# Two gather tiles in every three turns fetched row by row by SyncE and ScalarE

## What is computed

```python
# layer 0, for every edge e with source src[e] and destination dst[e]
w   = silu(edge_attr_64 @ fc_w1 / 8) @ fc_w2 / 8      # 224 weights for one edge
es, ev = h_s[edge_src], h_v[edge_src]                 # gathered node rows (64 + 96 numbers)
m_s1 = w1 * es * e0; m_s2 = w4 * dot(ev, e1)          # products of weight, row and edge attributes
m_v1 = w2 * es * e1; m_v2 = w3 * ev * e0; m_v3 = w5 * cross(ev, e1)
agg = segment_sum(mid, edge_dst)                      # then lin2, gates, silu
# layer 1: gather x[edge_src], products with edge_attr_4, segment_sum, linear maps W1..W5, Ws, Wv
```

## Time and profile before

| | us |
|---|---|
| median of three runs | 2017.59 |
| the profiled execution | 2016.04 |
| its span | 2014.2 |
| POOL busy in the span | 1459.9 (72%) |
| PE busy | 1695.3 (84%) |
| DVE busy | 1277.7 (63%) |
| ACT busy | 174.8 (9%) |

### The profile page before, as it was taken

The page is one execution under the profiler, slowest core; times in us unless marked ns, Lnnn a source line. Parts: engine busy times, 40 slices in busy tenths (PEclk is TensorE's granted clock), DMA queues, the critical chain, the costliest instruction groups (busy, mean ns, idle before and its releaser), DMA issues.

```text
span 2014.2 us, 41903 instructions
## 1 busy us (share of the span) xinstructions
PE 1695.3 (84%) x15596; PEld 1443.5 (72%) x15596; DVE 1277.7 (63%) x2725; ACT 174.8 (9%) x392; POOL 1459.9 (72%) x1558
## 2 busy tenths in 40 slices
PE   6989898989898989898958877878787878778786
PEld 4767676767676767676737877878787878778786
DVE  6787878787878877878875545444444545454443
ACT  5100000000000000000050000000000000000000
POOL 2777777777777777777737777777777777777774
PEclk9999999989999989989968989899998989899998
DMA  6333333333333333333322222222222223222223
GB/s 234 104 104 89 100 98 100 98 100 97 99 99 99 98 99 99 98 99 99 100 60 70 72 68 70 69 71 68 71 68 70 69 70 71 68 71 69 70 68 83
DMA packets 106120, 176.80 MB, mean 88 GB/s; under 512 B 27328, under 2 KB 73104, under 8 KB 105952
## 3 DMA queue, kind: packets, MB, share of 16 engines
q0 software_dynamic: 73200, 125.03, 25.5%
q1 hardware_dynamic: 30560, 49.88, 7.6%
q10 hardware_dynamic: 2320, 1.44, 0.2%
HBM read 170.10 MB, written 6.14 MB: 87 GB/s over the span
## 4 chain that ended last, share of the span: by engine, by line
POOL 69%; issue 22%; PE 4%; DVE 2%; DMA 1%; ACT 1%; POOLq 1%; DVEq 0%; ACTq 0%
POOL g L594 69%; PE sums L847 1%; PE w_ps L858 1%; DMA g<-node_table,src 1%; PE sums L868 1%; PE w_ps L457 1%; ACT H L268 0%; POOLq L589 0%; PE sums L858 0%; PE w_ps L812 0%; DMA node_table<-H 0%; PE w_ps L1020 0%; DVE work L721 0%; DMA ident_sb<-ident_dram 0%; PE sums L843 0%
## 5 line engine op out<-in xcount | busy, mean ns | idle before, releaser
L594 POOL DMA_INDIRECT g<-node_table,src x1525 | 1445.2, 948 | 494.8 <-issue 462.4
L847 PE MATMUL sums<-g,sel 128*128 128x160 f32 x1612 | 294.7, 344 | 178.7 <-DMA g<-node_table,src 177.4
L847 PEld LDWEIGHTS sums<-g,sel 128*128 128x128 f32 x1612 | 270.1, 223 | 195.9 <-DMA g<-node_table,src 139.9
L858 PE MATMUL w_ps<-H,work 128*128 128x160 f32 x2900 | 405.2, 300 | 2.5 <-DVE work L688 2.5
L858 PEld LDWEIGHTS w_ps<-H,work 128*128 128x128 f32 x2900 | 398.0, 191 | 2.7 <-DVE work L688 2.7
L721 DVE TENSOR_TENSOR work<-w_ps,g 128x384 f32<-128x384 f32 (+3 forms) x693 | 299.0, 459 | 114.5 <-DMA g<-node_table,src 67.7
L740 DVE STREAM_TRANSPOSE turned<-sums 128x160 f32<-128x160 f32 x232 | 80.1, 345 | 440.3 <-PE sums L868 303.5
L812 PE MATMUL w_ps<-fc_sb,work 64*128 64x224 f32 x1612 | 241.8, 398 | 89.2 <-DVE work L715 87.0
L843 PEld LDWEIGHTS sums<-work,sel 128*32 128x32 f32 x6448 | 202.6, 114 | 115.1 <-issue 78.0
L812 PEld LDWEIGHTS w_ps<-fc_sb,work 64*128 64x128 f32 x1612 | 173.2, 200 | 139.5 <-DVE work L715 120.4
L671 DVE TENSOR_TENSOR sel<-mixed,sh 128x896 f32<-128x896 f32 x232 | 251.7, 1085 | 28.9
(11 more groups left out here) (81 smaller groups left out, 536.3 us busy)
## 6 DMA issues: line engine op xcount, KB each, us to landing
feat<-edge_feat_dram SPq DMA_DIRECT2D x60, 512.0 KB
g<-node_table,src POOLq DMA_INDIRECT x1525, 2.6
named<-src_rows_dram SPq DMA_DIRECT2D x30, 128.0 KB, 3.0
X<-x_dram SPq DMA_DIRECT2D x5, 400.0 KB, 6.9
node_table<-H SPq DMA_DIRECT2D x5, 400.0 KB, 2.7
named<-src_rows_dram SPq DMA_DIRECT2D x30, 64.0 KB
sh<-edge_sh_dram SPq DMA_DIRECT2D x1, 1624.0 KB, 8.8
out_dram<-X SPq DMA_DIRECT2D x4, 240.0 KB, 3.3
```

Source lines behind the costliest of these rows:

```text
L594: nc.gpsimd.indirect_dma_start(out=g[:, u, j, :], out_offset=None, in_=table[layer], in_offset=bass.IndirectOffsetOnAxis(ap=src[:, at:at + ...
L847: last = nc.tensor.matmul(sums[:, o % 2, 0:D], sel[:, o % 2, j, :], g[:, o % UNROLL, j, :], **first_last)
L858: last = nc.tensor.matmul(found_at[:, i, 0:D], match[layer][:, i, t, :], H[:, t, :], start=(t == 0), stop=(t == NT - 1))
```

## The change

- Turns are taken in periods of three. The first two turns (`LEAD`) stand alone, then come nine periods (`PERIODS`), whose three turns (p = 0, 1, 2) stand in one loop body.
- In the turns p = 0 and p = 1 GpSimd no longer gathers the last tile of group 3. That of p = 0 is fetched by SyncE and that of p = 1 by ScalarE: 128 direct DMAs each, one for a row of 640 bytes, whose address comes from a register. The registers are loaded eight at a time from a row of node numbers in SBUF (`by_row`), which one small DMA brings for each period.
- `g` has two tiles more (30). `slot` places the tiles of group 3 so that the two row-fetched tiles have places of their own, which stay free to be filled for the turns in which they aren't used.
- SyncE spreads its 128 rows over the three turns as 48, 48 and 32 (`PARTS`), a quarter of them ahead of the load of the wanted numbers, the others between the two feature loads. ScalarE issues 12 rows at the end of nearly every stage (`SHARES`); in layer 0 the last eight come at the end of stage 3 of the very turn in which they are used.
- VectorE (layer 0) waits ahead of the second half of group 3's products until all 128 rows have landed, TensorE (layer 1) ahead of the last tile of group 3.
- The loop counter of `passes` now counts passes, not turns; `sync_picks` and `sync` are one function.

```diff
+PERIOD = 3
+LEAD = ITERS % PERIOD
+PERIODS = ITERS // PERIOD
+ROW_TILES = (2, 2)
+PARTS = (48, 48, 32)
+SHARES = ((0, 12, 12, 12) + (12,) * 4 + (12, 12, 12, 8), (12,) * 8 + (12, 12, 8, 0))
+AT_ONCE = 8
...
-        g = sb("g", [P, UNROLL, TILES, D])
+        g = sb("g", [P, UNROLL * TILES + 2, D])
...
+            def slot(p, u, j):
+                if u == UNROLL - 1 and j >= CHUNKS[1][0] and 0 <= p < ROW_TILES[layer]:
+                    n = j - CHUNKS[1][0]
+                    return (UNROLL * TILES - 3 + 2 * n) if p == 0 else (UNROLL * TILES - 2 + n)
+                return u * TILES + j
+            def fetch_rows(eng, which, i, a, b):
+                to = slot(i, UNROLL - 1, TILES - 1)
+                for c in range(a, b, AT_ONCE):
+                    d = min(c + AT_ONCE, b)
+                    _, nodes = nc.values_load_multi_w_load_instructions(by_row[i][0:1, c:d], engines=(which,), min_val=0, max_val=N - 1,
+                                                                        skip_runtime_bounds_check_because=LOAD_CHECK)
+                    for k, node in zip(range(c, d), nodes):
+                        eng.dma_start(g[k:k + 1, to, :], table[layer][bass.ds(node, 1), :]).then_inc(row_landed[i], 16)
+            def sync_turn(sp, f, it, part, e, k):
+                a, b = sum(PARTS[:part]), sum(PARTS[:part + 1])
+                some = a + (b - a) // 4
+                if part == 0:
+                    begin_rows(sp, 0, f, e, not isinstance(k, int))
+                fetch_rows(sp, mybir.EngineType.SP, 0, a, some)
+                more_rows(sp, f, it)
+                more_feat(sp, f, it, 0)
+                fetch_rows(sp, mybir.EngineType.SP, 0, some, b)
+                more_feat(sp, f, it, 1)
+                if part == PERIOD - 1:
+                    load_by_row(sp, 0, k + 1)
...
-                    tiles = min(tiles_of(UNROLL * it + u), by_pool[u])
+                    p = (it - LEAD) % PERIOD if it >= LEAD else -1
+                    tiles = min(tiles_of(UNROLL * it + u), by_pool[u] - by_row_at(p, u, TILES - 1))
...
+                def row_part(f, it, o, s, p, e, k):
+                    part = (p + 1) % PERIOD
+                    tile = e if part else e + 1
+                    n = part * UNROLL + o
+                    shares = SHARES[layer]
+                    a, b = sum(shares[:n]), sum(shares[:n + 1])
+                    if b > a == 0:
+                        begin_rows(act, 1, f, tile, p >= 0)
+                    fetch_rows(act, mybir.EngineType.Activation, 1, a, b)
+                    if b > a and b == P:
+                        load_by_row(act, 1, k + 1)
...
                     if o % UNROLL == own_weights and (s is None or s >= UNROLL):
                         copy(f, 1 if o >= UNROLL else 0)
+                    row_part(f, it, o, s, p, e, k)
...
                     elif u in picked:
                         dve.wait_ge(found_copied, picks * f + (picked.index(u) + 1))
+                    elif by_row_at(p, u, TILES - 1):
+                        dve.wait_ge(row_landed[p], 16 * P * e + 16 * P)
```

More of the change, by code:

```diff
@@ L83, with build @@
 PICKED = ((2,), (0, 2))
-def build(nc, x, node_vec, src_idx, src_rows0, src_rows1, node_id, dst_idx, edge_sh, edge_feat, ident, iota, lin_sc, lin_sc_scale,
+PERIOD = 3
+LEAD = ITERS % PERIOD
+PERIODS = ITERS // PERIOD
+assert LEAD == PERIOD - 1
+ROW_TILES = (2, 2)
+PARTS = (48, 48, 32)
+SHARES = ((0, 12, 12, 12) + (12,) * 4 + (12, 12, 12, 8), (12,) * 8 + (12, 12, 8, 0))
+AT_ONCE = 8
+assert all(sum(n) == P for n in (PARTS, *SHARES))
+LOAD_CHECK = "a transfer with a computed address is checked against the table's end"
+def build(nc, x, node_vec, src_idx, src_rows0, src_rows1, src_by_row, node_id, dst_idx, edge_sh, edge_feat, ident, iota, lin_sc, lin_sc_scale,
           fc1, fc2, big0, big0_scale, l1_pair, l1_pair_scale, l1_out, l1_out_scale, out):
@@ L182, in build @@
         named_in = [sem(f"named_in{l}") for l in range(2)]
+        by_row_in = [[sem(f"by_row_in{l}{i}") for i in range(2)] for l in range(2)]
         big0_in = sem("big0_in")
@@ L490, in edge_layer @@
             named_read = sem(L + "named_read")
+            row_landed = [sem(L + f"row_landed{i}") for i in range(2)]
             match_done = sem(L + "match_done")
@@ L520, in pass_over, with stages @@
                 eng.sem_inc(pass_left, 1)
[L522 to L528, removed]
+            def stages(eng, r, stage, last):
+                q = eng.snap(ITERS * r)
+                e = eng.snap(PERIODS * r + 0) - 1
+                for it in range(LEAD):
                     f = eng.snap(q + it)
                     for o in range(UNROLL):
[L531 to L534, removed]
@@ L548, in more_rows @@
[L548 to L563, removed]
+                        stage(f, it, o, UNROLL * it + o, it - LEAD, e, -1)
@@ new lines, in stages @@
+                with eng.Fori(0, PERIODS - 1) as k:
+                    e = eng.snap(PERIODS * r + k)
+                    for p in range(PERIOD):
+                        it = eng.snap(PERIOD * k + (LEAD + p))
+                        f = eng.snap(q + it)
+                        for o in range(UNROLL):
+                            stage(f, it, o, None, p, e, k)
+                e = eng.snap(PERIODS * r + (PERIODS - 1))
+                for p in range(PERIOD):
+                    it = ITERS - PERIOD + p
+                    f = eng.snap(q + it)
+                    for s in range(UNROLL * it, UNROLL * (it + 1) if p < PERIOD - 1 else last):
+                        stage(f, it, s - UNROLL * it, s, p, e, PERIODS - 1)
@@ L704, in products @@
                     w = w_ps[:, h, 0:n, :]
-                    rows = g[:, u, a:b, :]
+                    at = [slot(p, u, j) for j in range(a, b)]
+                    rows = g[:, at[0]:at[-1] + 1:at[1] - at[0] if n > 1 else 1, :]
                     to = prod[:, o % 2, a:b, :]
```

140 lines of the change are left out of this document (87 added, 53 removed).

## The result

The changed kernel takes 2077.27 us (median of 4 runs, 2070.6 to 2085.43) where the kernel before takes 2017.49 in the same job: ratio 1.0298, 95% interval 1.0249 to 1.0348. The direction was forecast, and the time lies in the range, but +60 us is twice the +28.5 forecast. The profiled execution has a span of 2082.1 us, 67.9 above the one before; it is one of the two longer of the four runs (two took 2070.6, two 2083.9 and 2085.4).

The account below looks back on a forecast made before the run. GpSimd's gather was taken as the bound, other engines 7% below in layer 0. Layer 0 +44 and layer 1 -22.5 gave 2039 us; half a row step more gave 2054; forecast 2046 between them, range 1971 to 2100.

Parts of the forecast that it names:

- Gather and layer 1: GpSimd: each gathered tile costs 1.25 us; two fewer per period save 22.5 us in layer 1.
- the fourth rival: Small transfers slow every gather; a rise of 0.03 us each eats the gain; chance 0.04, within "same".
- One row: Issuing one row on its sequencer: DMA 0.333 us plus register operation, move and gaps, taken as 0.50 us.
- its registers: Register load for the row addresses: 0.302 us, charged once for up to eight rows.
- B: Time of a block of 12 rows on ScalarE's queue in layer 0: 12R + 2 x 0.302 = 6.6 us.
- R: Sequencer time per issued row, taken as 0.50 us; forecast turns from gain to loss at 0.47.
- The silu behind the lin2 copy: ScalarE, layer 0: group 3's silu starts about 3.8 us later, behind a block of rows.
- The wait for the last rows: VectorE, layer 0, turn p = 1: stalls 8.9 us once per period for ScalarE's last eight rows.
- The slip of the find: Layer 0: late silu delays hidden layer and find, 1.5 us in two turns per period; 2.0 at R = 0.52.
- Hidden work on SyncE: SyncE in layer 0: its rows fit between feature loads; cover is gone if a row takes over 0.77 us.
- small terms, under 2 us together: Addresses on VectorE, wider `g`, three-turn loop on engines not the bound, first period's fetch: under 2 us together.
- the rivals with a cheap or middling row: Cheap: R up to 0.37, 1973 us, chance 0.20. Middling: R 0.37 to 0.45, 1983 to 2003 us, chance 0.19.

Follow-up runs that it names:

- r12: Changed kernel with one row-fetched tile per period in layer 0 (SyncE's, none by ScalarE), two in layer 1: 1984.43 us, 0.9835 times the kernel before.
- r02: Changed kernel without any row-fetched tile in layer 0, layer 1 as changed: 1996.74 us, 0.9893 times the kernel before.
- load12_again: pe_short with up to twelve registers loaded by one call in place of eight: 2015.9 us, 0.9972 times the kernel before.
- pe_short: Changed kernel, but TensorE alone keeps its loop over single turns in layer 0: 2049.39 us, 1.0158 times the kernel before.
- r12_short: r12 with TensorE looping over single turns in layer 0: 1985.05 us, 0.9844 times the kernel before.
- shared_again: pe_short with ScalarE's layer 0 rows in uneven blocks and the last 28 given to SyncE: 1997.0 us, 0.9889 times the kernel before.

## Why the prediction came out as it did

- **Gather and layer 1, right.** 1.25 us a tile; layer 1 -22.6 where -22.5 was forecast; r12 and r02 land within 1.2 us of the sums. So the fourth rival, gathers slowed by the small transfers, is out: 948 ns before and after.
- **One row, too dear; its registers, far too cheap.** The DMA takes 0.229 and the row 0.42, not 0.333 and 0.50. The register load takes 0.72 for eight and 0.59 for four, not 0.302 each: I had charged the 0.302 us of VectorE's load for eight values at once. In a block, 12 x 0.42 + 1.31 = 6.35, and 6.68 from silu to silu, against a forecast B of 6.6. The two errors cancel, and that is luck: the forecast put the whole dispute on R, with the sign turning at R = 0.47, and by that R = 0.42 would have given a gain. The sign came out right only because the loads took what the rows had left. What decides is the block with its loads: load12_again, 0.35 us less in each, took some 37 us off pe_short and brought it 0.3% below its kernel before.
- **The silu behind the lin2 copy 3.8 us later, right.** 6.61 - 2.84 = 3.77.
- **The wait for the last rows, right.** 69.4/9 = 7.7 us in nine waits where 8.9 was forecast; the landing took 1.3 us and not 2.8, taken from loads of 64 to 128 KB.
- **The slip of the find, 1.5 to 2.0 us in two turns, right in size over the 31.4 that it was added to.** pe_short's turns without the wait are 34.1 and 32.7, 2.7 and 1.3 over 31.4; in load12_again 0.7 and 0.2. But 31.4 is no floor of the other engines' work: r12, r12_short and shared_again have turns of 30.4. Over that the slips would be 3.7 and 2.3. What sets 31.4 was not taken apart.
- **Hidden work on SyncE, right.** No engine waits for its rows or for features, and r12 shows no cost. Its row DMA takes 0.228 us beside 0.229 on ScalarE's queue. The Trainium skill ("Perfetto Trace Analysis", on the HWDGE instruction) has the generator locked for one issuer at a time; the traces show no price of it on SyncE's side. In layer 0 of r12 SyncE issues rows alone, and they take 0.234 us in the mean, as in the changed kernel, where ScalarE issues beside it. ScalarE's rows, 0.268 in the mean with a longest of 0.542, have no run in which they are alone. The two dear issues that the prediction gave for the lock, 0.56 and 0.78 us, are two of five: in the same first 4 us ScalarE's others beside SyncE's took 0.45, 0.46 and 0.53.
- **Failed: "the loop over three turns saves two branches in three on engines that aren't the bound", and with it "small terms, under 2 us together".** The body of three turns costs TensorE 4.0 us at each of seven branches back, 27.95 us in the trace and 27.9 in the time. By the forecast's own sum the chain through TensorE was the bound in layer 0 (106.2 us against GpSimd's 98.75), so the edit that made its body three times as long could not be priced as if TensorE had slack. The Trainium skill ("Runtime: NRT & Kernel Launch", on how instructions are fetched) says that a taken branch to code that is no longer held makes a fetch and stalls the engine; the trace agrees, with 3.90 us of idle and q8's 15 packets grown to 106, and pe_short undoes both.

With that term the forecast reads 2046 + 28 = 2074, against 2077.27 measured. The 0.55 for "slower" held; the rivals with a cheap or middling row fell, not because the row was dear (0.42, in the middling rival's range), but because the loads made up for it.

## What to carry to other kernels

A longer loop body is a cost on the engine that paces: look whether the branch back shows an "issue" wait there, and loop each engine over as little as its own work needs. Price work put on an idle queue by the urgent instruction that stands behind it, and count what feeds it (here the register loads) as well as the transfers; let each register load start on a multiple of four numbers. And test halves separately: with SyncE's tile alone in layer 0 the same idea gives 1984 us, with ScalarE's added it gives 2077.

## What the runs showed of the hardware

- A load of registers from SBUF takes 0.59 us for four, 0.72 for eight and 0.96 for twelve when it starts on a multiple of four numbers, and 1.87 to 2.06 us for eight when it doesn't: the start's place counts for more than the number loaded.
- A one-row DMA of 640 bytes holds its sequencer for 0.229 us, where one of 128 partitions takes 0.333, and its row was used 1.3 us after its issue began.
- TensorE's loop with a body of three turns stalled 3.3 to 4.7 us at each branch back, and with a body of one turn not at all (pe_short).
- SyncE's one-row DMAs took 0.234 us in the mean whether ScalarE issued rows beside it or not (r12, layer 0).
- On three chips with a granted clock of 0.79 to 0.80 the kernel before takes 2844 to 2930 us in place of 2018. In the versions traced there the gather still takes 0.95 us, TensorE stands still for 434 to 482 us with nothing to wait for ahead of the find, and load12_again's kernel goes from 0.997 times the kernel before to 1.107.
